# Moving a mask's round trip through DRAM to another queue, and two small operations across a block's border

## What is computed

```python
x = L0_attn_x
xn = _layernorm(x, axis=-1)
s = _L0_attn_ref(xn, ...)          # attention, + xn, layer norm with gamma, beta
g = _silu(_L0_ffn_ref(xn, ...))    # second norm, linear, two experts' gelu layers, linear, gelu
x = x + s * g
...
key_mask = jnp.sign(jnp.abs(jnp.sum(x, axis=-1)))
scores = jnp.where(key_mask[:, None, None, :] == 0, NEG, scores)
```

## Time and profile before

| | us |
|---|---|
| median of 3 runs | 526.83 (526.40 to 527.27) |
| the profiled execution | 526.47 |
| its span, first to last instruction | 524.7 |
| first block, until the last SP issue | 186.04 |
| TensorE idle around the border | 180.28 to 188.93 |
| TensorE busy, share of the span | 83% |
| VectorE busy, share of the span | 76% |
| mean granted TensorE clock | 0.942 of 2.4 GHz |

### The profile page before, as it was taken

How to read it: one execution, slowest core, us unless ns; L and a number is a source line. 1 busy time by engine, 2 the same in 40 slices (tenths; PEclk the granted TensorE clock), 3 DMA queues, 4 the chain that set the end, 5 groups by cost and what they waited for, 6 DMA issues and landing times.

```text
span 524.7 us, 10282 instructions
## 1 busy us (share of the span) xinstructions
PE 437.2 (83%) x3697; PEld 269.2 (51%) x3697; DVE 399.6 (76%) x976; ACT 302.1 (58%) x644; POOL 126.5 (24%) x346
## 2 busy tenths in 40 slices
PE   0049545999999559999999999999999999999980
PEld 0026334767667425555555556556556555555540
DVE  6989998899984267667977877877877877787606
ACT  0029134888787504556666567567567566666670
POOL 8000000000000021011155154164163163162281
PEclk9999957999999955899999999999999999999996
DMA  8900021244443200122312312213323213222000
GB/s 231 296 0 0 11 71 31 60 122 125 126 126 82 81 6 24 51 69 49 93 48 69 92 49 79 82 48 90 74 47 101 61 48 111 52 48 67 3 22 20
DMA packets 27433, 37.60 MB, mean 72 GB/s; under 512 B 5622, under 2 KB 19830, under 8 KB 27382
## 3 DMA queue, kind: packets, MB, share of 16 engines
q1 hardware_dynamic: 27382, 36.94, 25.9%
HBM read 25.91 MB, written 10.49 MB: 69 GB/s over the span
## 4 chain that ended last, share of the span: by engine, by line
PE 53%; DVE 9%; issue 1%; ACT 1%; DVEq 0%; ACTq 0%
PE banks L963 15%; PE banks L994 14%; PE banks L982 12%; PE banks L965 5%; PE banks L984 5%; DVE mx L816 5%; PE banks L1004 1%; DVE stats L863 1%; DVE aggr L867 1%; ACT pt L934 0%; DVE bits L69 0%; DVE seed L70 0%; PE banks L972 0%; DVE half L894 0%; DVE res L850 0%
## 5 line engine op out<-in xcount | busy, mean ns | idle before, releaser
L816 DVE TENSOR_REDUCE mx<-banks 128x1 f32<-128x384 f32 (+3 forms) x384 | 211.1, 597 | 63.6 <-PE banks L965 58.4
L934 ACT ACTIVATE pt<-banks 128x512 f32<-128x512 f32 (+2 forms) x384 | 184.8, 528 | 110.8 <-PE banks L984 99.9
L965 PE MATMUL banks<-causal,ident_b 128*128 128x128 bf16 x512 | 106.8, 228 | 0.0
L984 PE MATMUL banks<-causalT,ident_b 128*128 128x128 bf16 x512 | 103.8, 222 | 0.0
L963 PE MATMUL banks<-k_own,q_own 73*128 73x512 bf16 (+3 forms) x256 | 75.3, 331 | 11.2 <-DVEq L896 8.6
L994 PE MATMUL banks<-pt,vg 128*18 128x512 f32 (+3 forms) x1024 | 82.4, 440 | 0.5 <-ACT pt L934 0.5
L963 PE MATMUL banks<-w_room 73*128 73x512 bf16 (+3 forms) x256 | 69.0, 302 | 3.4 <-DVE mx L816 3.4
L982 PE MATMUL banks<-q_own,k_own 76*128 76x512 bf16 (+3 forms) x256 | 71.1, 310 | 0.0
L982 PE MATMUL banks<-w_room 76*128 76x512 bf16 (+3 forms) x256 | 67.7, 300 | 1.2 <-ACT pt L934 1.2
L726 POOL TENSOR_SCALAR mneg<-mx 128x16 f32<-128x16 f32 x32 | 8.1, 253 | 192.7 <-DVEq L824 192.7
L965 PEld LDWEIGHTS banks<-causal,ident_b 128*128 128x128 bf16 x512 | 52.1, 102 | 0.0
(11 more groups left out here) (155 smaller groups left out, 581.1 us busy)
## 6 DMA issues: line engine op xcount, KB each, us to landing
k_scratch<-parts SPq DMA_DIRECT2D x40, 128.0 KB, 2.4
q_own<-q_scratch SPq DMA_DIRECT2D x48, 96.0 KB
k_own<-k_scratch SPq DMA_DIRECT2D x48, 96.0 KB
w_room<-q_scratch SPq DMA_DIRECT2D x48, 96.0 KB
w_room<-k_scratch SPq DMA_DIRECT2D x48, 96.0 KB
q_scratch<-parts SPq DMA_DIRECT2D x24, 128.0 KB, 2.4
w_room<-in_w_dram SPq DMA_DIRECT2D x1, 2048.0 KB, 9.2
out_dram<-mixed SPq DMA_DIRECT2D x7, 256.0 KB, 2.5
```

The costliest lines, as they stand in the source:

```text
L816: ins = dve.tensor_reduce(mx[:, u % 2, heads[0]:heads[-1] + 1, q], banks[:, S0 + c % RING, 0:w * len(heads)].rearrange("p (h k) -> p h k", ...
L934: act.activation(weights(k, heads[0], len(heads)), banks[:, ST0 + j % RING, 0:(T - P * k) * len(heads)], ACT.Exp, scale=SCALE).then_inc(ex ...
L965: ins = mm(o[:, w - P:w], ident_b[:, :], causal[:, :], start=False, stop=True)
L984: ins = mm(o[:, 0:P], ident_b[:, :], causalT[:, :], start=False, stop=True)
```

## The change

Four things move, and nothing is computed in another way.

1. The mask's store, the wait for its landing and the four loads leave SP's queue. GpSimd issues them, at the end of its part of the first block, waits for the loads to land (on a semaphore of their own, `mask_in`), and then counts up the four semaphores that TensorE looks at.
2. TensorE transposes the mask right behind the value products of the last step, ahead of the expert products.
3. ScalarE copies it out right behind the values, ahead of the hidden layer's activations.
4. `half` and the clearing of the bank OT are done by VectorE at the end of the first block, behind the last gate, in the order clearing, `half`.

```diff
+    half = sb("half", [P, 2, C])
+    mask_in = sem("first_mask_in")
...
-    def load_mask(sp, b, par, g):
+    def load_mask(sp, b, par, g, done):
...
-                     src.unsqueeze(0).unsqueeze(0).broadcast_to([1, G, T])).then_inc(stack_in[par][g], 16)
+                     src.unsqueeze(0).unsqueeze(0).broadcast_to([1, G, T])).then_inc(done, 16)
...
-                sp.wait_ge(maskT_ready, 1)
-                sp.dma_start(mask_dram, maskT[:, :]).then_inc(mask_out, 16)
-                sp.wait_ge(mask_out, 16)
-                for g in range(NG):
-                    load_mask(sp, 0, 0, g)
                 sp.wait_ge(w2_done, B)
                 load_ones(sp, 1)
...
                 pool.sem_inc(bias_ready, 1)
+                pool.wait_ge(maskT_ready, 1)
+                pool.dma_start(mask_dram, maskT[:, :]).then_inc(mask_out, 16)
+                pool.wait_ge(mask_out, 16)
+                for g in range(NG):
+                    load_mask(pool, 0, 0, g, mask_in)
+                pool.wait_ge(mask_in, 16 * NG)
+                for g in range(NG):
+                    pool.sem_inc(stack_in[0][g], 16)
...
                 gate(tok, B - 1)
+                link(dve.memset(banks[:, OT, :], 0.0))
+                dve.wait_ge(rows_in, 16)
+                link(dve.tensor_scalar(half[:, :, :], rows_sb[:, 2:4, :], 0.5, None, ALU.mult))
...
                                    ACT.Relu).then_inc(vb_free, 1)
+                    if last:
+                        act.wait_ge(maskT_done, 1)
+                        act.activation(maskT[:, :], banks[:, TRX, :].bitcast(BF16)[0:NT, 0:P],
+                                       ACT.Copy).then_inc(maskT_ready, 1)
                     for h in range(2):
...
-                    if last:
-                        act.wait_ge(maskT_done, 1)
-                        act.activation(maskT[:, :], banks[:, TRX, :].bitcast(BF16)[0:NT, 0:P],
-                                       ACT.Copy).then_inc(maskT_ready, 1)
-                    else:
+                    if not last:
                         second_norm(tok, i + 1)
...
                     ins.then_inc(v_done, 1)
+                    if i == B - 1:
+                        pe.wait_ge(mask_ready, 1)
+                        pe.transpose(banks[:, TRX, :].bitcast(BF16)[0:NT, 0:P], mask_b[:, :],
+                                     ident_b[:, :]).then_inc(maskT_done, 1)
                     pe.wait_ge(xaT_ready, tok.next(xaT_ready))
...
-                    if i == B - 1:
-                        pe.wait_ge(mask_ready, 1)
-                        pe.transpose(banks[:, TRX, :].bitcast(BF16)[0:NT, 0:P], mask_b[:, :],
-                                     ident_b[:, :]).then_inc(maskT_done, 1)
                     for h in range(2):
...
-                link(dve.tensor_scalar(half[:, :, :], rows_sb[:, 2:4, :], 0.5, None, ALU.mult))
-                link(dve.memset(banks[:, OT, :], 0.0))
                 dve.sem_inc(s_free, RING)
```

More of the change, by code:

```diff
@@ L162, in load_ones @@
                      ones_b[:, :].unsqueeze(1).broadcast_to([PARTS, HEADS, T])).then_inc(ones_in[par], 16)
+    RING = 3
+    S0, ST0, OT, MISC = 0, RING, 2 * RING, 2 * RING + 1
     with ExitStack() as one:
@@ L628, in build_program @@
         KCHUNKS = [(TB - 1 - q, heads) for q, heads in SCHUNKS]
-        NCH, RING = len(SCHUNKS), 3
+        NCH = len(SCHUNKS)
         assert NCH % RING == 0
@@ L646, in build_program @@
         mixed = s2b("mixed", [P, TB, C])
-        half = s2b("half", [P, 2, C])
         stats = s2b("stats2", [P, TB, 6])
@@ L650, in build_program @@
         bits = s2b("bits", [P, TB])
-        S0, ST0, OT, MISC = 0, RING, 2 * RING, 2 * RING + 1
         mrow_in = [sem("mrow_in0"), sem("mrow_in1")]
@@ L677, in load @@
                     load_keys(sp, b, par, g)
-                    load_mask(sp, b, par, g)
+                    load_mask(sp, b, par, g, stack_in[par][g])
                 def batch(tok, b):
```

## The result

The changed kernel takes 521.58 us (median of 6 runs, 521.23 to 522.60) against 526.93 us (median of 6, 526.25 to 527.63) measured beside it. The ratio is 0.9911, with a 95% interval of 0.9899 to 0.9922: 4.1 to 5.3 us faster. The forecast was 522.3 us in a range of 517.0 to 525.2. The two profiled executions are 4.3 us apart (526.47 and 522.16, spans of 524.7 and 520.4 us).

The account below looks back on a forecast made before the run. Bound: TensorE idle 8.6 us at the block border, behind SP's arrival and VectorE's work. 182.38 + 0.48 + 0.35 + 0.2, release 0.78, product 0.20: 184.4 against 188.93, 4.5 off 526.83 gives 522.3; range 517.0 to 525.2.

Parts of the forecast that it names:

- Who arrives last: At the border between blocks: SP last before, by 3.7 us; VectorE last after at 183.4, SP by 182.75, GpSimd 178.4.
- The price of `half`: VectorE's `half` at the first block's end: 0.35 us, not its row's 1.24, taken as waiting beside GpSimd's memset.
- The hand-overs and the release: At the border: 0.2 us for two VectorE hand-overs, release 0.78 after the last arrival, first score product 0.20 later.
- the sum: First score product at 184.4 against 188.93: 4.5 us gained, bounds 3.4 and 5.5.
- ScalarE and TensorE: Last step: the earlier mask copy delays ScalarE by up to 0.25 us, covered by 0.3; both engines' effects set at nothing.
- the 0.1 named: Last step: moving TensorE's mask transpose from ahead of the sixteen products could give back 0.1 us; set at nothing.
- a sign of being wrong: ScalarE's last Gelu coming later than before would mean the mask copy's 0.25 us was not covered.
- GpSimd: Mask store, landing wait and four loads on GpSimd's queue end at 178.4, with 0.1 us for semaphores.
- The covered case: GpSimd's transfers stay hidden, as VectorE ends 5.0 us later; each of five issues may cost 1.0 more than SP's 0.6.
- What follows shifts whole: Behind the first score product, the second block runs as before, only earlier by the whole gain.
- The clock: TensorE's granted clock would still more likely than not fall to half in the 4.1 us hole, and return at the same work.
- the rival's mechanism: Clock stays full across the shorter hole: 4.2 us from the first group, 0.5 from the filling, 517.6 us; chance 0.15.

Follow-up runs that it names:

- a: Changed kernel with `half` and the bank's clearing put back behind the border, leaving only the mask's way changed: 522.30 us, 0.9919 of the kernel before.
- b: Kernel before, with only VectorE's clearing and `half` moved ahead of the border, behind the last gate: 524.17 us, 0.9961 of the kernel before.
- c: Changed kernel with VectorE's clearing and `half` ahead of the last gate instead of behind it: 520.09 us, 0.9880 of the kernel before.
- e: Changed kernel with VectorE's pair back behind the border and GpSimd's memset there held until `half` is done: 520.76 us, 0.9886 of the kernel before.
- d: Changed kernel with the mask stored and loaded by SP ahead of the last step's parts, none by GpSimd: 520.84 us, 0.9897 of the kernel before.
- h: Changed kernel with 8 memsets in GpSimd's queue ahead of the mask's store: 524.17 us, 0.9961 of the kernel before.
- i: Changed kernel with 16 memsets in GpSimd's queue ahead of the mask's store: 527.30 us, 1.0016 of the kernel before.
- f: Changed kernel with 16 unused TensorE products added at the end of the first block, in the border's hole: 521.19 us, 0.9893 of the kernel before.
- j: Changed kernel with VectorE's pair ahead of the last gate, 10 unused products in the hole, one behind each of the filling's 24 chunks: 513.68 us.
- k: Changed kernel with VectorE's pair ahead of the last gate and one unused product behind each of the filling's 24 chunks, none in the hole: 516.22 us.

## Why the prediction was right, step by step

- **Who arrives last.** Right: SP before; VectorE after, with SP done issuing at 182.05 and GpSimd earlier. Runs a and b show both parts, and c shows VectorE's pair to have been last by about 1.2 us.
- **The price of `half`.** 0.35 taken, 0.29 measured; run e shows that the 1.24 was the neighbour's. The mirror at the program's start was a weaker sign than it reads: GpSimd's fast cast (10.74, 0.40) had VectorE working beside it too, on a sum (10.18, 1.22), so the two rows differ in which work stood beside and not in whether any did.
- **The hand-overs and the release.** 0.2 taken for two hand-overs, 0.29 + 0.04 measured (gate to clearing, clearing to `half`). The release took 0.59 us from VectorE's end (183.57 to 184.16) and not SP's 0.78, and the product followed 0.11 later, not 0.20. These small misses leave 0.2: the border is 1.80 us, the sum had 184.4 - 182.38 = 2.02.
- **ScalarE and TensorE.** The mask's copy was covered. The second half of the hidden layer still held up TensorE's loading of weights by 0.18 us, but not its products. The new order gave back more than the 0.1 named, a term that the sum put at nothing: from the start of the values' copy to that of the sixteen products it is 2.48 us (172.01 to 174.49) against 2.74 before, and 0.31 less to the gate; b, which leaves that order as it was, has none of it. ScalarE's last work does start later than before (181.12 against 181.03), which the prediction called a sign of being wrong; but the whole step starts 0.40 later in this trace, and against `v_all` it comes earlier.
- **GpSimd.** Its loads take 0.50 us each to issue (2.02 for four), less than SP's 0.63; store and loads land after 1.8 and 2.1 us; at the same place in d SP's store needed 1.3. The last landing was at 178.9, not 178.3. The covered case held, but the cover was 4.1 and not 5.0: the 0.1 taken for the semaphores behind the last landing had no row, and h and i show 0.6 more for it than VectorE needs to reach the border. And h shows that a landing is not the constant that I priced.
- **What follows shifts whole.** It did: 4.66 us at the third unit, 4.45 behind the first group.
- **The clock.** It fell in the shorter hole too, as forecast. But the rival's mechanism was wrong, and so was its price. I let the hole decide; run f shows that the filling brings the clock down by itself. And keeping it up is worth 6.05 us in the trace, not 4.7: a first group at full clock without a previous one's values takes 8.29 us, and I had put it at the 9.1 of the later groups, and the filling gains 1.0 and not 0.5. The 6.05 is for c's kernel with the clock held up through the filling by added work; no run has the clock up without such work.
- **The size.** The border gives 4.75 us, the profiled executions 4.3, the ratio 4.7; the medians of those runs are 5.35 apart. The forecast's 4.5 lies among them, in part by luck: it took the border's gain 0.2 too small and left out the 0.31 of the last step. In the profiled executions these two gains (4.75 + 0.31) less the later start of the last step (0.40) and the longer first group (0.21) give 4.45, which is what VectorE's maxima show. Why the start and the first group vary from trace to trace was not tested.

## What to carry to other kernels

At a border that all engines pass, write down each engine's arrival, and ask of every piece of work whether its engine is the last: b's pair was free, the changed kernel's same pair cost 1.1 us, and in a wait of 4.4 us on its own queue (c) it was free again. A row's duration is its price only if nothing stood beside it: look for the same operation at another place before moving it. Where one engine waits for another in short steps, look at the granted clock too; here work of no use cost nothing in those waits and was worth more than the change itself.

## What the hardware showed that I had not expected

TensorE's clock stayed at half (1.2 GHz) for the whole filling although its records fill the time (14.68 of 14.70 us busy in the changed kernel). With the same chunks and a 0.22 us product added to each, it stayed at full (2.4 GHz) in j, and rose to it within the filling in k; without them it fell in f from full after 5.0 us of filling. At half clock the busy share of the records told nothing: 14.68 of 14.70 us did not bring the clock up in the changed kernel, 5.78 of 5.80 were followed by its rise in k. At full clock it differed: 3.57 of 4.50 us before the fall in f, 13.36 of 13.40 in j. The second surprise is the landing of small transfers: the border was released 2.38 us after the issue of four loads of 4 KB when nothing else moved (i), and 4.23 when SP's loads of ones were under way (h).
